# A two-block graph-attention kernel: another order for the first loads, splits and matmul passes, and twelve one-hots in two wide operations

## Chip, cores and metric

One Trainium2 chip, one core. The metric is the device time of one execution in microseconds (us). Before the change the median of 3 runs is 358.46 us (358.44 to 358.57).

## What is computed

The input is `x` (256 nodes x 768 features, float32) and 4096 edges as `src` and `dst`, sorted by `dst`. Two residual blocks follow one another, each `x = layernorm(x + block(x))`. Block 0 is a graph attention with 8 heads of 768 features and an elu behind it, then a second attention with one head. Block 1 is a 4-head attention, a layer norm, relu and residual product, then a one-head attention with the same.

```
def gat_conv(x, src, dst, W, a_src, a_dst, b, heads, out_ch):
    h = (x @ W).reshape(n, heads, out_ch)
    alpha_src = jnp.einsum('nhc,hc->nh', h, a_src)
    alpha_dst = jnp.einsum('nhc,hc->nh', h, a_dst)
    e = jax.nn.leaky_relu(alpha_src[src] + alpha_dst[dst], NEG_SLOPE)
    ...
    out = jax.ops.segment_sum(msg, dst, num_segments=n)
```

In block 0 the node itself is added as one more edge, in block 1 too. The kernel never gathers by edge. It counts once how many edges lead from node s to node d (a 256 x 256 matrix of counts), and does every attention as a dense softmax weighted with these counts.

## The kernel before

**Products in three passes.** Every float32 matrix product is made of three fp32r products: high part by high part (pass 0), high by low (pass 1) and low by high (pass 2). `product` (line 999) writes the matmuls of the passes that it is given; the tuples `ALL`, `FIRST_TWO` and `LAST_ONE` (line 526) name them. A weight chunk is 128 rows x 768 columns (384 KB). It is loaded into `raw`, a ring of three groups of two chunks. ACT copies its high part into `ring_hi` (`split_hi`, line 349), and DVE or POOL subtracts that from the raw chunk into `ring_lo` (`split_lo`, line 367). In the first phase DVE does this for chunks 0 to 3 and POOL for chunks 4 and 5; in all later phases POOL does all six. `x` is transposed on PE (`transpose_x`, line 1152), each third of its columns by itself; its high part is copied from PSUM by ACT (`input_hi`, line 700) and its low part is subtracted by DVE (`input_lo`, line 1449).

**Phases.** A phase is six chunks. Phase 0 projects `x` with head 0's weights, phase 1 with head 1's; then phases of the second attention's weights and of the next head's alternate in a loop. All order is written out by hand: each engine has one program and waits on semaphores. The engines run their programs strictly in this order.

**The start, engine by engine.**

- SP (line 560 on) issues the loads: chunk 0 of phase 0, the first third of `x`, `src`, `dst`, chunk 1, the second third, chunk 2, the last third, chunk 3, then chunks 4 and 5 as one load of 768 KB. The three loads of phase 1 follow (`load_phase`, line 540), each 768 KB: the first waits until DVE has subtracted chunk 1 (the group of `raw` is then free), the second for chunk 3, the third for POOL's chunk 5.
- PE (line 1148 on): 8 matmuls on zeros (`keep_warm`), the transposes of the first third of `x`, 2 more on zeros, then the six chunks of phase 0, with the other transposes ahead of chunks 1 and 2. Chunks 0 and 2 wait for their low part at once (`chunk`, line 1013) and do passes 0 and 1, then pass 2. Then come chunks 0 and 1 of phase 1, the counting of edges (`count_edges`, line 1184), the scores of head 0 and chunks 2 to 5 of phase 1. Ahead of the second half of the last of them stand the transposes of head 0's weights.
- ACT (line 705 on): high parts of the chunks as they land, the three `input_hi`, and twenty of the 32 step rows for the counting (`steps`, line 696), in pieces. Between them it issues two loads of the attention vectors (`load_att`, line 680) and one of a bias (line 720). Behind that come the high parts of phase 1's chunks 0 and 1 (line 839), four steps, the high part of head 0's features, chunks 2 and 3, six steps and chunks 4 and 5.
- DVE (line 1456 on): low parts of chunks 0 to 3 and of `x`, edge arithmetic, twelve steps (`late_steps`, line 1478), the 32 one-hots (`hots`, line 1460), then the dot products for head 0 (line 1504) and the unpacking of the counts (line 1677).
- POOL: constants, then the low parts of chunks 4 and 5 and of phase 1.

**Counting.** Edge tile t has 128 edges, one on each partition. Its one-hot row has, at the edge's `dst` modulo 128, a weight that says in which half of the nodes `dst` is; its step row says for each node whether it lies at or above `src`. The product of both over all 32 tiles, 257 columns wide, gives running sums whose differences are the packed counts. Before, the weight is in the one-hot, and the steps are +0.5 or -0.5 for t from 20 on:

```
dve.tensor_scalar(hot(t), iota_ps[:, 1:1 + P], row_of[:, t:t + 1], weight_of[:, t:t + 1], ALU.is_equal, ALU.mult)
dve.tensor_scalar(step(t), iota[:, :], edges_f[:, 0, t:t + 1], -0.5, ALU.is_ge, ALU.add)
```

Of the kernel before, what the change touches and what calls it, by code (L numbers as in the profile page):

```python
# [22 lines left out]
ALU = mybir.AluOpType  # L23
# [94 lines left out]
def build_gnn(nc, x, src, dst, b0_W1, b0_as1, b0_ad1, b0_b1, b0_W2, b0_as2, b0_ad2, b0_b2,  # L118
# [5 lines left out]
    with ctx:  # L124
# [96 lines left out]
        STEPS_EARLY = 5  # L221
# [8 lines left out]
        single_loaded = [sem(f"single_loaded{c}") for c in range(2)]  # L230
# [118 lines left out]
        def split_hi(eng, p, c, reused=True):  # L349

            if p is FIRST_PHASE and c in (0, 2):
                eng.wait_ge(single_loaded[c // 2], 16)
            elif c % 2 == 0 or p is FIRST_PHASE and c in (1, 3):
                eng.wait_ge(raw_full[c // 2], 16 * p + 16)
# [177 lines left out]
        def _(sp):  # L532
# [26 lines left out]

            sp.dma_start(raw[:, 0, 0:D], w1[:, 0, 0, :]).then_inc(single_loaded[0], 16)  # L560
            load_x(0)
            sp.dma_start(edges[:, 0, :], src.rearrange("(p t) -> p t", p=P)).then_inc(edges_loaded, 16)
            sp.dma_start(edges[:, 1, :], dst.rearrange("(p t) -> p t", p=P)).then_inc(edges_loaded, 16)
            sp.dma_start(raw[:, 0, D:2 * D], w1[:, 1, 0, :]).then_inc(raw_full[0], 16)
# [4 lines left out]
            load(0, 2, w1_of(0)(2))  # L569
# [109 lines left out]
        def _(act):  # L679
            def load_att(n, a_src, a_dst, width, reused=True):  # L680

                if reused:
                    act.wait_ge(a_dst_done, 2 * n)
# [23 lines left out]
            input_hi(0)  # L707
            split_hi(act, FIRST_PHASE, 1, reused=False)
            act.wait_ge(iota_cast, 1)
            act.wait_ge(src_biased, 1)  # L710
            steps(0, 3)
            split_hi(act, FIRST_PHASE, 2, reused=False)
            input_hi(1)
            steps(3, 5)
            split_hi(act, FIRST_PHASE, 3, reused=False)
            input_hi(2)
            load_att(0, b0_as1[0:1, :], b0_ad1[0:1, :], D, reused=False)
            split_hi(act, FIRST_PHASE, 4, reused=False)
# [274 lines left out]
        def _(pe):  # L993
# [26 lines left out]
            def keep_warm(times, at):  # L1020


                for _ in range(times):
                    pe.matmul(ps[:, at:at + BANK], zeros[:, 0:P], zeros[:, :], start=True, stop=True)
# [124 lines left out]
            keep_warm(8, PROJ)  # L1149
# [11 lines left out]
            keep_warm(2, PROJ + 2 * BANK)  # L1161
            for c in range(CH):
                if c == 2:
# [864 lines left out]
```

## Time and profile before

| what | value |
|---|---|
| median of 3 runs | 358.46 us |
| the profiled execution's own time | 358.43 us |
| its span in the profile | 356.6 us |
| PE busy | 347.9 us, 98% of the span |
| DVE, ACT, POOL busy | 213.4, 218.5 and 242.4 us |
| DMA | 65.15 MB, 183 GB/s over the span |

The profile is of one execution. The span goes from its first to its last instruction; 1.8 us of the execution's own time lie around it. Starts below are counted from the start of the span. "Idle" in a row is the time that the engine stood still just ahead of it, with the instruction or load that ended it.

### The profile page before, as it was taken

What the parts mean: (1) busy time and instruction counts of PE and PEld (TensorE: products, weight loads), DVE (VectorE), ACT (ScalarE), POOL (GpSimd) and SP (SyncE); (2) the same over time, 40 slices, a digit from 0 to 9 for tenths busy, and PEclk for the clock granted to TensorE, in tenths of its full rate; (3) what the DMA queues carried; (4) which work ended last, traced back from release to release, by engine and by line L of the source; (5) the groups of instructions that cost most, each with busy time, mean ns of one, the idle gap of its engine ahead of it and who ended that gap; (6) DMA issues with size and microseconds to landing.
All of it is one profiled execution on the core that took longest, in us unless ns stands there. A gap on an engine that the chain in (4) does not pass through costs nothing.

```text
span 356.6 us, 6079 instructions
## 1 busy us (share of the span) xinstructions
PE 347.9 (98%) x2058; PEld 298.9 (84%) x2060; DVE 213.4 (60%) x545; ACT 218.5 (61%) x376; POOL 242.4 (68%) x163
## 2 busy tenths in 40 slices
PE   7999999999999999999999999999999999999994
PEld 4888889889888988988898898898667888788883
DVE  4999883263546418244552732636687897944776
ACT  5987697547737754864674575476376866255601
POOL 2379769657693884968569396674257898687911
PEclk9999999999999999999999999999999999999999
DMA  7987969576656556656574754757072656246002
GB/s 235 312 299 225 391 214 257 179 240 144 227 150 203 176 155 205 170 176 183 170 217 143 224 170 141 246 159 237 11 218 94 217 179 198 99 135 221 0 2 88
DMA packets 24544, 65.15 MB, mean 183 GB/s; under 512 B 1952, under 2 KB 3024, under 8 KB 24528
## 3 DMA queue, kind: packets, MB, share of 16 engines
q1 hardware_dynamic: 20864, 55.02, 47.0%
q10 hardware_dynamic: 3664, 9.92, 10.8%
q8 instruction: 9, 0.15, 0.2%
q14 instruction: 7, 0.06, 0.0%
HBM read 64.15 MB, written 0.79 MB: 182 GB/s over the span
## 4 chain that ended last, share of the span: by engine, by line
PE 92%; DVE 4%; ACT 1%; DMA 1%; issue 1%; DVEq 0%; SPq 0%
PE ps L1008 64%; PE ps L1298 10%; PE ps L1096 9%; PE ps L1130 2%; PE ps L1362 2%; PE ps L1075 1%; DMA x_sb<-in_x 1%; PE ps L1060 1%; PE ps L1192 1%; DVE stats L1744 1%; DVE ps L1964 1%; DVE z L1971 1%; PE ps L1157 0%; PE ps L1383 0%; PE ps L1310 0%
## 5 line engine op out<-in xcount | busy, mean ns | idle before, releaser
L370 POOL TENSOR_TENSOR ring_lo<-raw,ring_hi 128x768 fp32r<-128x768 f32 x92 | 167.0, 1849 | 70.9 <-ACT ring_hi L357 70.8
L357 ACT ACTIVATE ring_hi<-raw 128x768 fp32r<-128x768 f32 x96 | 77.3, 839 | 35.7 <-PE ps L1008 28.8
L386 POOL TENSOR_TENSOR ring_lo<-raw,ring_hi 128x512 fp32r<-128x512 f32 (+1 forms) x40 | 59.5, 1517 | 20.3 <-ACT ring_hi L379 20.2
L1008 PE MATMUL ps<-ring_hi,zT_hi 128*128 128x256 f32 (+1 forms) x256 | 69.3, 345 | 0.4 <-ACT zT_hi L808 0.4
L1008 PE MATMUL ps<-ring_lo,zT_hi 128*128 128x256 f32 (+1 forms) x256 | 67.1, 337 | 0.0
L1008 PE MATMUL ps<-ring_hi,zT_lo 128*128 128x256 f32 (+1 forms) x256 | 66.8, 338 | 0.0
L1515 DVE CUSTOM_DVE_ANT_0 e<-ps,att 128x768 f32<-128x768 f32 x38 | 34.3, 953 | 47.6 <-PE ps L1008 47.6
L1008 PE MATMUL ps<-ring_hi,xT_hi 128*128 128x512 f32 x192 | 51.2, 343 | 0.3 <-ACT xT_hi L702 0.3
L1008 PE MATMUL ps<-ring_lo,xT_hi 128*128 128x512 f32 x192 | 50.0, 336 | 0.0
L1008 PE MATMUL ps<-ring_hi,xT_lo 128*128 128x512 f32 x192 | 49.8, 337 | 0.0
L1008 PEld LDWEIGHTS ps<-ring_lo,zT_hi 128*128 128x128 f32 x256 | 43.0, 188 | 5.6
L1008 PEld LDWEIGHTS ps<-ring_hi,zT_lo 128*128 128x128 f32 x256 | 43.0, 188 | 5.5
L1008 PEld LDWEIGHTS ps<-ring_hi,zT_hi 128*128 128x128 f32 x256 | 42.0, 189 | 6.4 <-ACT zT_hi L808 1.0
L379 ACT ACTIVATE ring_hi<-raw 128x512 fp32r<-128x512 f32 (+1 forms) x40 | 26.5, 712 | 17.0 <-PE ps L1008 10.0
L1657 DVE SCALAR_TENSOR_TENSOR ps<-ps,b_plus,z 128x256 f32<-128x256 f32 x48 | 21.2, 487 | 25.9 <-ACT z L800 25.8
L1008 PEld LDWEIGHTS ps<-ring_hi,xT_hi 128*128 128x128 f32 x192 | 32.3, 188 | 5.0 <-ACT xT_hi L702 0.7
L1008 PEld LDWEIGHTS ps<-ring_lo,xT_hi 128*128 128x128 f32 x192 | 32.7, 188 | 4.2
L1008 PEld LDWEIGHTS ps<-ring_hi,xT_lo 128*128 128x128 f32 x192 | 32.6, 188 | 4.1
L1096 PE MATMUL ps<-pT_hi,h_hi 128*128 128x256 f32 x96 | 26.0, 282 | 0.0
L1096 PE MATMUL ps<-pT_hi,h_lo 128*128 128x256 f32 x96 | 26.0, 282 | 0.0
L1666 DVE SCALAR_TENSOR_TENSOR zT_lo<-ps,zT_hi 128x512 fp32r<-128x512 f32 x24 | 16.6, 691 | 15.3 <-ACT zT_hi L808 15.3
L794 ACT ACTIVATE z<-ps,b_minus 128x256 f32<-128x256 f32 x48 | 20.1, 471 | 6.2 <-PE ps L1096 6.2
(172 smaller groups left out, 545.4 us busy)
## 6 DMA issues: line engine op xcount, KB each, us to landing
raw<-in_L_gnn_W SPq DMA_DIRECT2D x54, 768.0 KB, 4.5
raw<-in_L_gnn_Wr SPq DMA_DIRECT2D x8, 768.0 KB, 4.3
att<-in_L_gnn_a_src ACTq DMA_DIRECT2D x10, 384.0 KB, 4.0
att<-in_L_gnn_a_dst ACTq DMA_DIRECT2D x10, 384.0 KB, 5.2
raw<-in_L_gnn_W SPq DMA_DIRECT2D x4, 384.0 KB, 5.0
x_sb<-in_x SPq DMA_DIRECT2D x3, 256.0 KB, 4.8
rows_hc<-in_L_gnn_b SPq DMA_DIRECT2D x1, 512.0 KB, 7.6
rows_hc<-in_L_gnn_g SPq DMA_DIRECT2D x1, 512.0 KB, 8.4
```

The costliest lines, as they stand in the source:

```text
L357: eng.activation(slot_hi(c), raw_chunk(c), ACT.Copy).then_inc(hi_done, 1)
L370: eng.tensor_tensor(slot_lo(c), raw_chunk(c), slot_hi(c).bitcast(F32), ALU.subtract)\
L379: eng.activation(ring_hi[:, q["ring_at"]:q["ring_at"] + w], raw[:, q["raw_group"], q["raw_at"]:q["raw_at"] + w], ACT.Copy)\
L386: eng.tensor_tensor(ring_lo[:, q["ring_at"]:q["ring_at"] + w], raw[:, q["raw_group"], q["raw_at"]:q["raw_at"] + w], ring_hi[:, q["ring_at" ...
L794: act.activation(z[:, t * N:(t + 1) * N], ps[:, at:at + N], ACT.Relu, bias=b1_minus[:, bass.ds(KD * h + t, 1)], scale=-1.0).then_inc(elu_r ...
L1008: last = pe.matmul(ps[:, at + to:at + to + hi - lo], a, b[:, lo:hi], start=start and n == 0 and to != D, stop=stop and n == PASSES - 1, sk ...
L1096: return pe.matmul(ps[:, at:at + N], feat(features, 0, j)[:, ch:ch + P], weights_part[:, 0, j, :], start=first, stop=final, skip_group_che ...
L1130: return pe.matmul(ps[:, nat_at[i] + lo:nat_at[i] + hi], weights_part[:, 0, j, i * P:(i + 1) * P], feat(features, a, j)[:, lo:hi], start=f ...
L1298: last = pe.matmul(ps[:, to:to + HW], a, b, start=k == 0 and n == 0, stop=k == KD - 1 and n == PASSES - 1, skip_group_check=True)
L1515: dve.tensor_tensor_reduce(junk[:, at:at + w], of[:, (k - first_head(a)) * w:(k - first_head(a) + 1) * w], att[:, half_at * row + k * w:ha ...
L1657: dve.scalar_tensor_tensor(ps[:, at:at + N], ps[:, at:at + N], b1_plus[:, bass.ds(KD * h + t, 1)], z[:, t * N:(t + 1) * N], ALU.add, ALU.m ...
L1666: dve.scalar_tensor_tensor(zT_lo[:, 2 * q:2 * q + 2, :].rearrange("p k n -> p (k n)"), ps[:, at:at + 2 * N], -1.0, hi.bitcast(F32), ALU.ad ...
```

## The change

It touches the first 25 us or so of every engine but POOL. SP loads the first third of `x` ahead of chunk 0, chunk 1 ahead of the edges, chunks 4 and 5 singly, and then the attention vectors, which ACT issued before. PE issues 5 wide matmuls on zeros ahead of the transposes and 2 wide ones and one of 256 columns behind them. Chunks 0, 1 and 2 do pass 0, then pass 2, then pass 1; for chunks 1 and 2 the next transposes stand behind pass 0, and the low part of the chunk is waited for only ahead of pass 1. The high part of `x`'s first third is copied by DVE. ACT does 2 steps ahead of chunk 4 and 8 behind chunk 5 (before: 3, 2 and 5). For t from 20 on the weight is in the step, a second operand read for each partition, and the one-hots of tiles 20 to 23 and 24 to 31 are one comparison each, a `tensor_tensor` over 4 x 128 and 8 x 128 elements. The late steps are 1, 2, 3 and 6 in place of 5 and 7. One more small operation prepares the weights.

```
-        STEPS_EARLY = 5
+        STEPS_EARLY = 3
+        BELOW_FROM = (ACT_STEPS + ET) // 2
+        PLAIN = ((ACT_STEPS, 24), (24, ET))
...
-            if p is FIRST_PHASE and c in (0, 2):
+            if p is FIRST_PHASE and c % 2 == 0:
                 eng.wait_ge(single_loaded[c // 2], 16)
-            elif c % 2 == 0 or p is FIRST_PHASE and c in (1, 3):
+            elif c % 2 == 0 or p is FIRST_PHASE:
                 eng.wait_ge(raw_full[c // 2], 16 * p + 16)
...
+            load_x(0)
             sp.dma_start(raw[:, 0, 0:D], w1[:, 0, 0, :]).then_inc(single_loaded[0], 16)
-            load_x(0)
+            sp.dma_start(raw[:, 0, D:2 * D], w1[:, 1, 0, :]).then_inc(raw_full[0], 16)
             sp.dma_start(edges[:, 0, :], src.rearrange("(p t) -> p t", p=P)).then_inc(edges_loaded, 16)
             sp.dma_start(edges[:, 1, :], dst.rearrange("(p t) -> p t", p=P)).then_inc(edges_loaded, 16)
-            sp.dma_start(raw[:, 0, D:2 * D], w1[:, 1, 0, :]).then_inc(raw_full[0], 16)
             load_x(1)
...
-            load(0, 2, w1_of(0)(2))
+            sp.dma_start(raw[:, 2, 0:D], w1[:, 4, 0, :]).then_inc(single_loaded[2], 16)
+            sp.dma_start(raw[:, 2, D:2 * D], w1[:, 5, 0, :]).then_inc(raw_full[2], 16)
+            for half_at, v in ((0, b0_as1), (1, b0_ad1)):
+                sp.dma_start(att[:, half_at * D:(half_at + 1) * D], v[0:1, :].partition_broadcast(P))\
+                  .then_inc(att_loaded, 16)
             load_phase(1, w1_of(1))
...
-            input_hi(0)
             split_hi(act, FIRST_PHASE, 1, reused=False)
+            split_hi(act, FIRST_PHASE, 2, reused=False)
+            input_hi(1)
+            split_hi(act, FIRST_PHASE, 3, reused=False)
             act.wait_ge(iota_cast, 1)
             act.wait_ge(src_biased, 1)
-            steps(0, 3)
-            split_hi(act, FIRST_PHASE, 2, reused=False)
-            input_hi(1)
-            steps(3, 5)
-            split_hi(act, FIRST_PHASE, 3, reused=False)
+            steps(0, 2)
+            split_hi(act, FIRST_PHASE, 4, reused=False)
             input_hi(2)
-            load_att(0, b0_as1[0:1, :], b0_ad1[0:1, :], D, reused=False)
-            split_hi(act, FIRST_PHASE, 4, reused=False)
             split_hi(act, FIRST_PHASE, 5, reused=False)
             act.dma_start(rows_d[:, 3, :], b0_b2.partition_broadcast(P)).then_inc(b2_loaded, 16)
-            steps(5, 10)
+            steps(2, 10)
...
-            keep_warm(8, PROJ)
+            keep_warm(5, PROJ)
...
             transpose_x(0)
             keep_warm(2, PROJ + 2 * BANK)
+            keep_warm(1, PROJ + 2 * BANK, N)
             for c in range(CH):
-                if c == 2:
+                if c == 3:
                     pe.wait_ge(b1_loaded, 16)
...
-                if c in (1, 2):
-                    transpose_x(c)
-                if c in (0, 2):
+                if c in (0, 1, 2):
                     pe.wait_ge(xT_hi_done, c // 2 + 1)
-                    chunk(FIRST_PHASE, c)
-                    for passes in (FIRST_TWO, LAST_ONE):
+                    pe.wait_ge(hi_done, c + 1)
+                    for passes in ((0,), LAST_ONE, (1,)):
                         if passes is LAST_ONE:
+                            if c > 0:
+                                transpose_x(c)
                             pe.wait_ge(xT_lo_done, c // 2 + 1)
+                        if passes == (1,):
+                            chunk(FIRST_PHASE, c)
...
+            def plain_hots(first, end):
+                at = (first % per_home) * 2 * N
+                home = hot_homes[first // per_home][:, at:at + (end - first) * 2 * N]
+                shape = [P, end - first, P]
+                dve.tensor_tensor(home.rearrange("p (t n) -> p t n", n=2 * N)[:, :, 0:P],
+                                  iota_ps[:, 1:1 + P].rearrange("p (t n) -> p t n", t=1).to_broadcast(shape),
+                                  row_of[:, first:end].rearrange("p (t n) -> p t n", n=1).to_broadcast(shape),
+                                  ALU.is_equal).then_inc(hot_done, 1)
...
+            dve.wait_ge(xT_ps, 1)
+            dve.tensor_copy(xT_hi[:, 0:2, :].rearrange("p k n -> p (k n)"), ps[:, XT_AT:XT_AT + BANK])\
+               .then_inc(xT_hi_done, 1)
+            input_lo(0)
             split_lo(dve, FIRST_PHASE, 0)
-            input_lo(0)
...
-            for at, end, scale in ((0, ACT_STEPS, 1.0), (ACT_STEPS, ET, 2.0)):
+            for at, end, scale in ((0, ACT_STEPS, 1.0), (ACT_STEPS, BELOW_FROM, 2.0), (BELOW_FROM, ET, -2.0)):
...
-                    dve.tensor_scalar(step(t), iota[:, :], edges_f[:, 0, t:t + 1], -0.5, ALU.is_ge, ALU.add)\
-                       .then_inc(step_dve_done, 1)
+                    dve.tensor_scalar(step(t), iota[:, :], edges_f[:, 0, t:t + 1], weight_of[:, t:t + 1],
+                                      ALU.is_lt if t >= BELOW_FROM else ALU.is_ge, ALU.mult).then_inc(step_dve_done, 1)
...
-            hots(0, ET)
+            hots(0, ACT_STEPS)
+            for first, end in PLAIN:
+                plain_hots(first, end)
```

## Rows read from the trace of the kernel before

**Rows 1.** The page: busy time, share of the span and instructions by engine.

```profile
PE 347.9 (98%) x2058; PEld 298.9 (84%) x2060; DVE 213.4 (60%) x545; ACT 218.5 (61%) x376; POOL 242.4 (68%) x163
```

**Rows 2.** Chain that ended last, in order of time: start us, us, what.

```profile
1.19 3.88 DMA x_sb<-in_x
...
12.34 12.58 PE ps L1008 x72
```

**Rows 3.** Timeline, head: start us, us, engine, line, operation, tiles, count, idle.

```profile
1.31 3.59 PE L1024 MATMUL ps<-zeros 128*128 128x512 bf16 x8 [1.31 <-POOL zeros L601]
...
4.37 0.84 ACT L357 ACTIVATE ring_hi<-raw 128x768 fp32r<-128x768 f32 x1 [2.13 <-DMA raw<-in_L_gnn_W]
...
5.20 0.72 PE L1157 MATMUL ps<-ident,x_sb 128*128 128x128 f32 x4 [0.30 <-DMA x_sb<-in_x]
...
5.76 0.59 PE L1024 MATMUL ps<-zeros 128*128 128x512 bf16 x2
5.96 0.60 ACT L702 ACTIVATE xT_hi<-ps 128x512 fp32r<-128x512 f32 x1 [0.76 <-PE ps L1157]
...
6.62 0.62 PE L1008 MATMUL ps<-ring_hi,xT_hi 128*128 128x512 f32 x2 [0.26 <-ACT xT_hi L702]
...
7.07 0.51 PE L1008 MATMUL ps<-ring_lo,xT_hi 128*128 128x512 f32 x2
```

**Rows 4.** Timeline, PE: first matmuls of phase 1 and of the counting.

```profile
20.55 0.51 PE L1008 MATMUL ps<-ring_hi,xT_hi 128*128 128x512 f32 x2
...
24.76 1.05 PE L1192 MATMUL ps<-am 128*128 128x257 bf16 x8
```

**Rows 5.** Timeline, ACT and POOL: last splits of phase 0, steps, first of phase 1.

```profile
14.03 0.83 ACT L357 ACTIVATE ring_hi<-raw 128x768 fp32r<-128x768 f32 x1
...
14.28 7.26 POOL L370 TENSOR_TENSOR ring_lo<-raw,ring_hi 128x768 fp32r<-128x768 f32 x4 [11.00 <-ACT ring_hi L357]
...
14.77 1.30 ACT L698 ACTIVATE am<-iota,src_bias 128x257 bf16<-128x257 bf16 x3
...
16.77 1.56 ACT L357 ACTIVATE ring_hi<-raw 128x768 fp32r<-128x768 f32 x2
```

**Rows 6.** DMA issues: chunk 3 (at 4.57), phase 1's first (at 9.17): us to landing.

```profile
raw<-in_L_gnn_W SPq DMA_DIRECT2D x1, 384.0 KB, 6.3
...
raw<-in_L_gnn_W SPq DMA_DIRECT2D x1, 768.0 KB, 5.6
```

**Rows 7.** Windows: us, busy time by engine, PEclk, DMA share, GB/s.

```profile
4.50:5.00 0.50, 0.41 (x1) 0.00 (x0) 0.00 (x0) 0.50 (x1) 0.00 (x0) 1.00 0.90 156
...
12.00:13.00 1.00, 1.00 (x10) 0.91 (x8) 1.00 (x7) 0.70 (x2) 0.00 (x0) 1.00 1.03 409
...
15.00:16.00 1.00, 1.00 (x8) 0.89 (x7) 1.00 (x5) 1.00 (x4) 1.00 (x1) 1.00 0.89 135
16.00:17.00 1.00, 1.00 (x7) 0.85 (x6) 1.00 (x5) 1.00 (x4) 1.00 (x2) 1.00 1.02 187
...
39.00:40.00 1.00, 1.00 (x10) 1.00 (x10) 1.00 (x3) 0.78 (x2) 1.00 (x1) 1.00 1.03 422
```

**Rows 8.** DMA issues: second attention vector (at 12.77): us to landing.

```profile
att<-in_L_gnn_a_dst ACTq DMA_DIRECT2D x1, 384.0 KB, 7.0
```

**Rows 9.** Groups by line and shape, DVE: busy us, mean ns.

```profile
L1693 DVE TENSOR_SCALAR far<-ps 128x256 f32<-128x256 f32 x2 | 0.8, 418 | 0.0
...
L1622 DVE TENSOR_SCALAR am<-ps,rz 128x256 f32<-128x256 f32 x16 | 7.0, 479 | 0.3
...
L1451 DVE TENSOR_TENSOR xT_lo<-ps,xT_hi 128x512 fp32r<-128x512 f32 x3 | 2.1, 685 | 0.4 <-ACT xT_hi L702 0.4
```

**Rows 10.** Timeline, DVE: last one-hots, first dot product, first unpacking step.

```profile
19.77 5.19 DVE L1462 TENSOR_SCALAR rows_hc<-ps,row_of,weight_of 128x128 bf16<-128x128 f32 x16
...
24.88 0.95 DVE L1515 CUSTOM_DVE_ANT_0 e<-ps,att 128x768 f32<-128x768 f32 x1
...
29.25 0.41 DVE L1677 SCALAR_TENSOR_TENSOR hs<-hs,ps 128x256 f32<-128x256 f32 x1
```

More of the change, by code:

```diff
@@ L229, in build_gnn @@
         chunk_used = sem("chunk_used")
-        single_loaded = [sem(f"single_loaded{c}") for c in range(2)]
+        single_loaded = [sem(f"single_loaded{c}") for c in range(RG)]
         x_loaded = [sem(f"x_loaded{b}") for b in range(3)]
@@ L679, in _, with load_att @@
         def _(act):
-            def load_att(n, a_src, a_dst, width, reused=True):
-                if reused:
-                    act.wait_ge(a_dst_done, 2 * n)
+            def load_att(n, a_src, a_dst, width):
+                act.wait_ge(a_dst_done, 2 * n)
                 for half_at, v in ((0, a_src), (1, a_dst)):
@@ L1018, in node_tile, with keep_warm @@
                 return t[:, k, i * P:(i + 1) * P]
-            def keep_warm(times, at):
+            def keep_warm(times, at, width=BANK):
                 for _ in range(times):
-                    pe.matmul(ps[:, at:at + BANK], zeros[:, 0:P], zeros[:, :], start=True, stop=True)
+                    pe.matmul(ps[:, at:at + width], zeros[:, 0:P], zeros[:, 0:width], start=True, stop=True)
             def project_chunk(p, h, c, loop=False, at=PROJ, between=None):
@@ L1186, in count_edges @@
                 for t in range(ET):
-                    pe.wait_ge(hot_done, t + 1)
+                    pe.wait_ge(hot_done, t + 1 if t < ACT_STEPS else ACT_STEPS + sum(first <= t for first, _ in PLAIN))
                     if t < ACT_STEPS:
@@ L1479, in late_steps @@
                 for t in range(first, end):
-                    dve.tensor_scalar(step(t), iota[:, :], edges_f[:, 0, t:t + 1], -0.5, ALU.is_ge, ALU.add)\
-                       .then_inc(step_dve_done, 1)
+                    dve.tensor_scalar(step(t), iota[:, :], edges_f[:, 0, t:t + 1], weight_of[:, t:t + 1],
+                                      ALU.is_lt if t >= BELOW_FROM else ALU.is_ge, ALU.mult).then_inc(step_dve_done, 1)
             split_lo(dve, FIRST_PHASE, 1)
             dve.wait_ge(iota_cast, 2)
-            late_steps(ACT_STEPS, ACT_STEPS + STEPS_EARLY)
+            dve.wait_ge(edges_split, 5)
+            late_steps(ACT_STEPS, ACT_STEPS + 1)
             split_lo(dve, FIRST_PHASE, 2)
             input_lo(1)
-            late_steps(ACT_STEPS + STEPS_EARLY, ET)
+            late_steps(ACT_STEPS + 1, ACT_STEPS + STEPS_EARLY)
             split_lo(dve, FIRST_PHASE, 3)
+            late_steps(ACT_STEPS + STEPS_EARLY, ACT_STEPS + 2 * STEPS_EARLY)
             input_lo(2)
+            late_steps(ACT_STEPS + 2 * STEPS_EARLY, ET)
             dve.wait_ge(b1_ps, 1)
@@ L1494, in _ @@
                .then_inc(b1_ready, 1)
-            dve.wait_ge(edges_split, 4)
-            hots(0, ET)
+            hots(0, ACT_STEPS)
+            for first, end in PLAIN:
+                plain_hots(first, end)
             def dots_scale(a, half_at, i):
```

## Prediction

> **What bounds the kernel now.** Read first the page's busy times: PE is busy for 98% of the span [rows 1], so nothing but less work or less standing on PE can shorten it. PE's work stays the same but for 2.5 matmuls on zeros, which stand ahead of the first product. So the question is how much earlier PE gets through the head, and whether it keeps that. The chain that ended last starts with the load of `x`'s first third, issued at 1.19 us and landed 3.88 us later, at 5.07, and from 12.34 on it is PE without a gap [rows 2]. The timeline of the head shows what lies between: transposes at 5.20, the copy of their high part on ACT at 5.96 for 0.60 us, the first product at 6.62 [rows 3]. Chunk 0 itself had landed at 4.37, when ACT started its split. So the first product waits for `x`, not for the weights. Further marks are PE's start of phase 1 at 20.55 and of the counting at 24.76 [rows 4]. For what PE would meet if it came earlier I read ACT and POOL [rows 5] and the DMA issues and windows [rows 6 to 8].
>
> **Step 1, the first product: 0.65 us earlier.** `x`'s first third and chunk 0 change places. Together they have landed at 5.07 now, so chunk 0 as the second should land at about 5.07. Its split takes 0.84 us, to 5.91, and PE follows its releaser by 0.06 (5.96 + 0.60 = 6.56, against 6.62) [rows 3]: 5.97. The other leg must be no later. 256 KB cannot land later than 384 KB in the same place do, at 4.37. Plus 0.13 to the transposes (5.07 to 5.20), 0.76 to the copy (5.20 to 5.96), and the copy on DVE. No row has this copy; DVE's subtraction of the same 512 columns takes 685 ns [rows 9] and reads one tensor more, so I take 0.69, with ACT's 0.60 as the near bound. That is 5.95 at the latest, so the leg is covered. The low parts come in the order `x` (to about 6.6), then chunk 0 (to about 7.5); PE wants them one and two passes in, at 6.8 and 7.5. That is even, because the pass that needs the later one comes last. Three matmuls fewer on zeros cost nothing in themselves; see the clock below.
>
> **Step 2, PE from there to phase 1: 0.10 us longer.** Now 13.93 us lie between the first product and phase 1 (6.62 to 20.55). A pair of matmuls that starts after something else takes 0.45 us (6.62 to 7.07) in place of 0.35 [rows 3]. The transposes inside chunks 1 and 2 make such a restart each, as the ones ahead of them do now; the bias transpose, now next to the last ones, gets a restart of its own. So 14.03, and PE is at phase 1 at 20.00 instead of 20.55: 0.55 earlier. Chunks 3 to 5 are covered by what step 3 works out for ACT: chunk 3 is split from 10.5 on, so its low part is ready near 12.7 and wanted near 13.7; POOL's two are ready near 14.7 and 16.5 and wanted near 15.8 and 17.9.
>
> **Step 3, ACT and POOL up to phase 1: just in time.** PE needs the low part of phase 1's chunk 0. ACT starts its high part at 16.77 [rows 5], and POOL does its four low parts in 7.26 us, so in 1.82 each, the third ready at 19.75. After the change ACT has eight steps behind chunk 5 in place of five. Its work from chunk 3 on: split 0.74 (14.03 to 14.77), two steps at 0.40 (five take 14.77 to 16.77), split 0.74, copy 0.60, split 0.74, eight steps 3.20: 6.82 in all. Chunk 3 now lands at 4.57 + 6.3 = 10.87 [rows 6]. The same bytes stand ahead of it afterwards, but the DMA engines have a dip to 156 GB/s at 4.5 to 5.0 us [rows 7], while the two small edge loads pass, and large loads stood behind these. With chunk 1 ahead of them part of the dip is filled. Bounds: nothing gained, 10.87, or the dip's whole 0.7 us, 10.2; I take the middle, 10.5. Then phase 1's first split starts at 17.3, POOL can begin at 18.15 and has done at 20.0. PE arrives at 20.0, so I charge 0.08. With the bounds it is nothing to 0.45.
>
> **Step 4, the load of phase 1.** It is issued at 9.17 and lands 5.6 us later, at 14.77 [rows 6], two microseconds ahead of its use. Now 768 KB of attention vectors go ahead of it in SP's own queue. At 409 GB/s (12 to 13 us) that is 1.9 us; at the 135 and 187 GB/s of 15 to 17 us, when those vectors move now [rows 7], it is 4.9. So it lands between 14.77 + 1.9 - 0.3 (half the dip) = 16.4 and 19.4. SP's own broadcasts of the later bias rows run at 422 GB/s at 39 to 40 us [rows 7], so I take the near end plus 0.6, a part of the 0.9 us that a third 384 KB takes, for the bias load from ACT beside it, 17.0: ahead of ACT's 17.3, free. The attention vectors themselves, landed at 12.77 + 7.0 = 19.8 now [rows 8], are wanted at about 23.6, and ACT saves two issues in its program.
>
> **Step 5, the counting.** DVE has run without idling from 7.2 us to the first unpacking step at 29.25 and stands in the way of the head's softmax, which PE reaches just in time. It loses twelve one-hots at 5.19/16 = 0.32 us [rows 10], 3.89 us, and gains two wide comparisons. The nearest row is the subtraction of 512 elements, 0.69 [rows 9]; two to three times that for 512 and 1024 elements together is 1.4 to 2.1, and I take 1.8. The second operand per partition makes each late step longer: 479 ns with one against 418 with none on the same shape [rows 9], 0.06, or 0.7 us for twelve (bounds: 0 and 0.1 each). The third weight operation adds 0.1. Net 3.9 - 1.8 - 0.7 - 0.1 = 1.3 us earlier: one-hots end at 23.6 instead of 24.9, and all DVE does behind them can follow. That covers PE's gain; without the wide ones DVE would now be 0.8 late and PE would wait for it. ACT's last steps need 17.3 + two splits 1.5 + four steps 1.6, then the features behind chunk 5, 1.5, two splits, 1.5, six steps, 2.4: 25.8. PE wants the last at about 26.4. Covered.
>
> **Sum.** 0.65 - 0.10 - 0.08 = 0.47 us at phase 1. I take off 0.1 for small new waits behind it, and all that comes later is a chain on PE which shifts as a whole. Against the profiled execution's 358.43 that gives 358.06; the median stands 0.03 above it. Forecast: **358.1 us**. A measurement of this kernel tells about 0.2%, 0.72 us, from no change, so this is within it.
>
> **Rival 1, slower: the load of phase 1 lands late.** If the vectors move at the slow rate of 15 to 17 us, the load lands at 18.8 or later instead of 17.0. From 17.3 on each 0.1 us of it is 0.1 on ACT, POOL and PE. At 17.8 the gain is gone; at 18.8 PE starts phase 1 at 18.8 + 0.84 + 1.84 + 0.06 = 21.5, 1.0 later than now: 359.4 us. For it: 135 GB/s at a DMA share of 0.89 [rows 7]. Against it: in those windows they go through the other queue. The Trainium skill (DMA: Bandwidth & Descriptors, Queues, rings and completion order) says that each engine takes its queues in turn and drains one queue in order; by that rule the vectors, until now beside SP's loads, are ahead of them, and the trace agrees so far, since phase 1's first load lands ahead of both vectors now.
>
> **Rival 2, slower: the clock comes later.** The eight matmuls of 512 columns on zeros start 0.43 us apart, 512 at 1.2 GHz; the two at 5.76 are at 0.21, so at 2.4 GHz [rows 3]. PE had then worked from 1.31 to 4.90 and again from 5.20. Afterwards the zeros end at about 3.6, PE stands until about 4.2, and works again. If the clock is still at 1.2 GHz at the first product, a pass costs 1.28 us (two node tiles of 768 columns) instead of 0.70: for chunk 0's three passes 1.7 us, so 359.8; with two passes it is already 0.2% slower than now. The Trainium skill (TensorE: Matmul & The Clock Gate, Part 1) says the array is throttled by default, that sustained activity releases it, and that the moment varies from run to run, which speaks against cutting the work on zeros. The four times before lie within 0.14 us, which does not show such a variation.
>
> **Rival 3, nothing moves.** The gain of the head is swallowed by chunk 3 landing at 10.87 and by POOL: PE waits 0.45 at phase 1, 358.3 to 358.5. **Rival 4, more:** the second landing is earlier, the dip is filled, and PE's small stutters go as well: 0.8 to 1.0, 357.5.
>
> **Chances.** Forecast 0.50, of which 0.08 may lie beyond 0.72 us; rival 1 0.18 (half of it over 0.2% slower), rival 2 0.13 (0.10 over it), rival 3 0.11, rival 4 0.08 (all faster). Faster 0.16, slower 0.19 and 0.02 for mishaps, 0.21; within 0.2% 0.63. The range leaves out the far ends of rivals 1 and 2 and of 4: 357.5 to 359.2.
>
> **What would show it.** Right: first product at about 5.95, phase 1 on PE near 20.1, counting near 24.3, dot products on DVE near 23.6, no PE wait over 0.2 us, everything behind shifted by 0.4. Wrong: matmuls 0.43 us apart beyond 6 us (rival 2); ACT idle for the weights near 17 us and PE idle at phase 1 (rival 1); late steps well over 0.34 us or the wide comparisons over 2.1 us together, with PE waiting in the counting; or a PE gap behind 30 us.

## The result, and the profile after

The changed kernel takes 360.26 us (median of 6 runs, 359.97 to 361.14), the kernel before 358.61 beside it (6 runs, 358.44 to 358.74). The ratio is 1.0048, 95% interval 1.0036 to 1.0061: slower by 1.7 us. The forecast was 358.1, in a range of 357.5 to 359.2. The profiled execution took 360.47 us.

The page of the changed kernel, busy times and the chain that ended last:

```profile
span 358.7 us, 6069 instructions
...
PE 347.9 (97%) x2056; PEld 299.0 (83%) x2058; DVE 215.4 (60%) x537; ACT 218.2 (61%) x375; POOL 242.6 (68%) x163
...
PE 84%; DVE 11%; ACT 2%; DMA 1%; issue 1%; DVEq 0%; SPq 0%
```

PE's work is what it was, 347.9 us [rows 1]. But DVE has 2.0 us more work. It should have had 0.6 less: the forecast's 1.3 us, less the 0.7 of the copy of `x`'s first third, which it takes over from ACT. Its share of the last chain is 11%. In the kernel before it was 4%, and PE had the chain without a gap from 12.34 to 24.92 [rows 2] and on to the transposes of head 0's weights. A line of its page, and one of its timeline:

```profile
PE 92%; DVE 4%; ACT 1%; DMA 1%; issue 1%; DVEq 0%; SPq 0%
...
36.04 0.60 PE L1075 MATMUL ps<-ident,am 128*128 128x128 f32 x4
```

Which of PE's waits is new? The waits of the changed kernel, costliest first:

```profile
PE ps L1078 <- DVE am L1645: 1.4, 1, 1.4
PE ps L1027 <- POOL zeros L609: 1.3, 1, 1.3
PE ps L1012 <- ACT ring_hi L361: 0.8, 1, 0.8
```

The first is new and carries the loss: PE stands 1.4 us ahead of the transposes of head 0's weights, which DVE's softmax delivers. The chain from there back, in order of time (start, us, what):

```profile
11.88 0.86 DVE ring_lo L374
12.74 2.31 DVE rows_hc L1499 x3
15.05 0.59 DVE xT_lo L1457
15.65 2.51 DVE rows_hc L1499 x6
...
18.38 2.55 DVE am L1478 x8
```

Line 1499 is a late step of the counting. Three take 2.31 us and six take 2.51; before, five took 1.07 and seven 1.47. The timeline of the head, DVE, POOL and PE:

```profile
12.66 2.40 DVE L1499 TENSOR_SCALAR rows_hc<-iota,edges_f,weight_of 128x257 bf16<-128x257 bf16 x3
14.97 0.68 DVE L1457 TENSOR_TENSOR xT_lo<-ps,xT_hi 128x512 fp32r<-128x512 f32 x1
15.57 2.59 DVE L1499 TENSOR_SCALAR rows_hc<-iota,edges_f,weight_of 128x257 bf16<-128x257 bf16 x6
...
24.66 1.84 DVE L1471 TENSOR_TENSOR rows_hc<-ps,row_of 128x512 bf16<-128x512 f32 x2
26.38 0.97 DVE L1538 CUSTOM_DVE_ANT_0 e<-ps,att 128x768 f32<-128x768 f32 x1
...
13.06 3.72 POOL L374 TENSOR_TENSOR ring_lo<-raw,ring_hi 128x768 fp32r<-128x768 f32 x2 [9.76 <-ACT ring_hi L361]
18.14 3.65 POOL L374 TENSOR_TENSOR ring_lo<-raw,ring_hi 128x768 fp32r<-128x768 f32 x2 [1.36 <-ACT ring_hi L361]
...
6.53 0.94 PE L1012 MATMUL ps<-ring_hi,xT_hi 128*128 128x512 f32 x4 [0.80 <-ACT ring_hi L361]
...
24.66 1.05 PE L1198 MATMUL ps<-am 128*128 128x257 bf16 x8
...
37.52 0.66 PE L1078 MATMUL ps<-ident,am 128*128 128x128 f32 x4 [1.43 <-DVE am L1645]
```

Both slow groups lie beside POOL's pair of subtractions, 13.06 to 16.78. In the kernel before the late steps stood here:

```profile
9.06 1.07 DVE L1480 TENSOR_SCALAR rows_hc<-iota,edges_f 128x257 bf16<-128x257 bf16 x5
...
11.60 1.47 DVE L1480 TENSOR_SCALAR rows_hc<-iota,edges_f 128x257 bf16<-128x257 bf16 x7
```

The last of them ended at 13.07 (11.60 + 1.47), and POOL's first subtraction started at 14.28 [rows 5]: they never met. In single instructions (min/median/max) the twelve are

```profile
L1499 DVE TENSOR_SCALAR rows_hc<-iota,edges_f,weight_of x12: 342/347/1883, 9.0 to 17.8; 128x257 bf16<-128x257 bf16 x12
```

Ten take 0.35 us, one takes 1.88 (issued at 13.17, 0.1 us after POOL began) and one 1.30 (issued at 15.57, ending at 16.87, 0.1 us behind POOL's second subtraction). That is 1.53 + 0.95 = 2.5 us too much. DVE reaches its first dot product at 26.38 instead of 24.88 [rows 10], 1.50 later, the weights' transposes start at 37.52 instead of 36.04, 1.48 later, and PE does not make it up. Theory A: **a late step that meets a subtraction of POOL stands until that ends, inside its own recorded duration**, and DVE's lateness becomes PE's.

### The profile page after: what moved, and what is told of

It is laid out like the page before. It is cut to its first block, busy times and chain, and to the rows that moved or that the text cites. A ratio compares the mean times of both kernels' runs of the same rounds, so it can differ in the third digit from the quotient of the medians.

```text
span 358.7 us, 6069 instructions
## 1 busy us (share of the span) xinstructions
PE 347.9 (97%) x2056; PEld 299.0 (83%) x2058; DVE 215.4 (60%) x537; ACT 218.2 (61%) x375; POOL 242.6 (68%) x163
## 4 chain that ended last, share of the span: by engine, by line
PE 84%; DVE 11%; ACT 2%; DMA 1%; issue 1%; DVEq 0%; SPq 0%
PE ps L1012 58%; PE ps L1304 10%; PE ps L1099 9%; PE ps L1133 2%; PE ps L1368 2%; PE ps L1078 2%; DVE rows_hc L1499 1%; DMA raw<-in_L_gnn_W 1%; PE ps L1063 1%; DVE e L1538 1%; DVE stats L1767 1%; DVE am L1478 1%; DVE z L1478 1%; DVE ps L1987 1%; DVE z L1994 1%
## 5 line engine op out<-in xcount | busy, mean ns | idle before, releaser
L383 ACT ACTIVATE ring_hi<-raw 128x512 fp32r<-128x512 f32 (+1 forms) x40 | 26.5, 713 | 17.1 <-PE ps L1012 10.3
```

The costliest lines, as they stand in the source:

```text
L383: eng.activation(ring_hi[:, q["ring_at"]:q["ring_at"] + w], raw[:, q["raw_group"], q["raw_at"]:q["raw_at"] + w], ACT.Copy)\
```

## The experiments

Each ran beside the kernel before on its chip. "Dots" is the start of DVE's first dot product; "1.0028 [1.0018, 1.0038]" is a ratio to the kernel before, with its 95% interval.

**e1: the late steps read the copy of the node numbers in PSUM.** All else is the changed kernel.

```
-                    dve.tensor_scalar(step(t), iota[:, :], edges_f[:, 0, t:t + 1], weight_of[:, t:t + 1],
+                    dve.tensor_scalar(step(t), iota_ps, edges_f[:, 0, t:t + 1], weight_of[:, t:t + 1],
```

> The changed kernel, with the twelve late steps reading the row of node numbers from its PSUM copy instead of SBUF. Theory A (a late step reads and writes SBUF in a fast form that cannot run beside POOL's SBUF subtraction, and waits until that one ends): read from PSUM no late step is longer than 0.6 us, the 1.88 and 1.30 us ones are gone; each costs some 0.20 us more by itself (a 257-column PSUM operation took 0.42, plus two operands of 0.06), so 2.4 us are added where 2.5 go, the dot products start near 26.3 us as now, and the time stays at 360.0 to 360.5. Theory B (the long steps come from something else: the second operand, or the DMA writes into SBUF): the two long ones stay at 1.9 and 1.3, 2.4 us come on top, 362 to 363.

360.0 us, 1.0028 [1.0018, 1.0038]. The line of the late steps (instructions: min/median/max ns, first and last start), and two rows of the timeline:

```profile
L1499 DVE TENSOR_SCALAR rows_hc<-ps,edges_f,weight_of x12: 540/544/549, 8.9 to 17.0; 128x257 bf16<-128x257 f32 x12
```

```profile
12.96 3.65 POOL L374 TENSOR_TENSOR ring_lo<-raw,ring_hi 128x768 fp32r<-128x768 f32 x2 [9.68 <-ACT ring_hi L361]
14.71 2.81 DVE L1499 TENSOR_SCALAR rows_hc<-ps,edges_f,weight_of 128x257 bf16<-128x257 f32 x6
```

Beside the same pair of subtractions no step is long. All cost 0.54 instead of 0.35 for the other source, so more than half of the loss stays: dots at 25.76. The copy in PSUM is float32 and the one in SBUF bfloat16, so this edit changes place and type at once; which of the two frees the step is not shown.

**e2: the old one-hots and the old late steps, in the new places.** The hunks of the diff on `plain_hots`, `weight_of` and `late_steps` are undone; the order stays.

> The changed kernel with the old one-hots (32 narrow, weighted) and the old steps (one operand per partition and -0.5), in the new places. Theory A (waiting for POOL): two of the late steps still take 1.9 and about 1.3 us, the others 0.28; DVE loses the 1.3 us that the wide ones save, the dot products start near 27.7 and the time is 361.2 to 361.9. Theory B (the second operand is what makes late steps long): all late steps take 0.28, the dot products start near 25.2, 358.6 to 359.2.

363.8 us, 1.0151 [1.0125, 1.0177]. The steps have a minimum of 0.28, a median of 0.29 and a maximum of 1.89 us; the long ones start at 14.34 (0.98) and 15.23 (1.89), beside POOL's pair at 13.37. So the long steps come from the place, not from the second operand. Dots are at 28.27. The time is above what was expected, since DVE is now so late that PE waits in three more places: 1.5 us for the scores, 1.3 for the next phase's input, 0.5 for POOL.

**e3: the late steps kept clear of POOL.** Two, one and three ahead of the low part of chunk 3, six behind the seventh one-hot, between POOL's two pairs.

```
-            late_steps(ACT_STEPS, ACT_STEPS + 1)
+            late_steps(ACT_STEPS, ACT_STEPS + 2)
             split_lo(dve, FIRST_PHASE, 2)
+            late_steps(ACT_STEPS + 2, ACT_STEPS + 3)
             input_lo(1)
-            late_steps(ACT_STEPS + 1, ACT_STEPS + STEPS_EARLY)
+            late_steps(ACT_STEPS + 3, ACT_STEPS + 6)
             split_lo(dve, FIRST_PHASE, 3)
-            late_steps(ACT_STEPS + STEPS_EARLY, ACT_STEPS + 2 * STEPS_EARLY)
             input_lo(2)
-            late_steps(ACT_STEPS + 2 * STEPS_EARLY, ET)
...
-            hots(0, ACT_STEPS)
+            hots(0, 7)
+            late_steps(ACT_STEPS + 6, ET)
+            hots(7, ACT_STEPS)
```

> The changed kernel with its late steps where POOL stands: 2, 1 and 3 of them ahead of chunk 3's low part, which ends as POOL starts, and 6 behind the seventh one-hot, in POOL's pause from 16.8 to 18.1 us. Theory A: at most one step over 0.5 us, dot products start near 24.0 us instead of 26.4, PE no longer waits 1.4 us at the transposes of head 0's weights, the time is 358.3 to 358.7, so that of the kernel before. Theory B (the late steps or the wide comparisons cost too much in themselves, wherever they stand): 360 or more. If the order of loads and passes at the head was a gain in itself, it shows here as less than 358.4.

358.48 us, 0.9985 [0.9976, 0.9994]. Repeated as e14 below: 0.9986. Its late steps by line, and its timeline:

```profile
L1499 DVE TENSOR_SCALAR rows_hc<-iota,edges_f,weight_of x12: 341/346/349, 8.8 to 17.7; 128x257 bf16<-128x257 bf16 x12
```

```profile
16.44 1.64 DVE L1499 TENSOR_SCALAR rows_hc<-iota,edges_f,weight_of 128x257 bf16<-128x257 bf16 x6
...
18.08 3.64 POOL L374 TENSOR_TENSOR ring_lo<-raw,ring_hi 128x768 fp32r<-128x768 f32 x2 [1.42 <-ACT ring_hi L361]
...
23.86 0.95 DVE L1539 CUSTOM_DVE_ANT_0 e<-ps,att 128x768 f32<-128x768 f32 x1
24.29 1.05 PE L1198 MATMUL ps<-am 128*128 128x257 bf16 x8
```

The same twelve instructions take 3.5 us in all in place of 5.9, dots start 2.5 earlier than in the changed kernel, the new wait of PE is gone, and the time falls by 2.2 us, to below the kernel before. The place of the late steps alone makes the difference between a loss and a gain. The first of the six still starts 0.22 us ahead of the end of POOL's first pair (14.82 + 1.84), but it is no longer than the others: it ends at 16.78, 0.1 behind POOL.

**e4: the kernel before with the wide comparisons and the weighted steps, all else in its old place.**

```
-            hots(0, ET)
+            hots(0, ACT_STEPS)
+            for first, end in PLAIN:
+                plain_hots(first, end)
```

(The hunks on `plain_hots`, `weight_of` and the steps themselves, as in the change, are left out here.)

> The kernel before with only the DVE part of the change: weight in the late steps, twelve one-hots in two comparisons, the late steps in their old places (5 and 7), all of them ahead of POOL's first subtraction at 14.3 us. Theory A: no long step, the dot products start near 23.6 instead of 24.9, PE does not need them earlier, time unchanged within 0.2 us of 358.6. If instead DVE was what PE waited for in the head: up to 1 us faster.

359.02 us, 1.0003 [0.9994, 1.0012]. Steps 346 to 354 ns, dots at 23.57, 1.3 us earlier than in the kernel before; DVE then stands 1.49 us ahead of its first unpacking step. PE does not gain, as it was bound by its own work.

**e5: the kernel before with seven of its late steps moved behind the low part of `x`'s last third.** Nothing of the change is in it.

```
-            late_steps(ACT_STEPS + STEPS_EARLY, ET)
             split_lo(dve, FIRST_PHASE, 3)
             input_lo(2)
+            late_steps(ACT_STEPS + STEPS_EARLY, ET)
```

> The kernel before, with one thing moved: its seven late steps stand behind the low part of x's last third, so from about 13.1 us on, and run into POOL's run of four subtractions from 14.3 to 21.5 us; nothing else is changed and the work is the same. Theory A (a late step that meets a running POOL subtraction waits for its end): three or four steps fit ahead of 14.3, each later one is let in at one of POOL's boundaries (16.1, 17.9, 19.8, 21.5), so three or four steps of 1.0 to 1.9 us, DVE 5 to 6 us late at its dot products (near 30 us), PE waits for the one-hots, the scores and the weights, 363 to 365 us. Theory B (the order of DVE's work does not matter, or the long steps need the changed kernel's second operand or its DMA traffic): all steps 0.28 us, 358.9 to 359.3, as the kernel before.

364.54 us, 1.0154 [1.0137, 1.0171]. Its line of the late steps and the timeline, with the single ones cut out of their group:

```profile
L1480 DVE TENSOR_SCALAR rows_hc<-iota,edges_f x12: 283/291/1898, 9.2 to 18.2; 128x257 bf16<-128x257 bf16 x12
```

```profile
16.38 1.90 DVE L1480 TENSOR_SCALAR rows_hc<-iota,edges_f 128x257 bf16<-128x257 bf16 x1
18.20 1.88 DVE L1480 TENSOR_SCALAR rows_hc<-iota,edges_f 128x257 bf16<-128x257 bf16 x1
...
16.34 1.84 POOL L370 TENSOR_TENSOR ring_lo<-raw,ring_hi 128x768 fp32r<-128x768 f32 x1
18.15 1.83 POOL L370 TENSOR_TENSOR ring_lo<-raw,ring_hi 128x768 fp32r<-128x768 f32 x1
```

The two long steps shown start 0.04 to 0.05 us behind a subtraction and end 0.1 behind its end. Back to back, POOL lets one step in for each of its own. Three such steps (14.57, 16.38, 18.20) put dots at 30.38, 5.5 us late, and the time is 5.55 above the kernel before: one for one. The two subtractions shown are 1.83 and 1.84 us, no longer than elsewhere (mean 1.85). As the loads are those of the kernel before, the changed order of the DMAs is no cause of the long steps either.

**e6, e7, e8: the other parts of the change, one undone at a time, on top of e3.** e6 loads the edges ahead of chunk 1 again, e7 has eight wide matmuls on zeros in front again, e8 lets ACT issue the attention vectors again, behind the high part of `x`'s last third.

```
-            sp.dma_start(raw[:, 0, D:2 * D], w1[:, 1, 0, :]).then_inc(raw_full[0], 16)
             sp.dma_start(edges[:, 0, :], src.rearrange("(p t) -> p t", p=P)).then_inc(edges_loaded, 16)
             sp.dma_start(edges[:, 1, :], dst.rearrange("(p t) -> p t", p=P)).then_inc(edges_loaded, 16)
+            sp.dma_start(raw[:, 0, D:2 * D], w1[:, 1, 0, :]).then_inc(raw_full[0], 16)
```

> The kernel with late steps clear of POOL, and the two edge loads issued ahead of chunk 1, as in the kernel before. If chunk 0 lands late because chunk 1 follows it directly and shares the DMA engines: chunk 0 lands 0.3 to 0.5 us earlier (3.6 us after issue or less), chunk 1 about 0.5 later, first product near 5.7; chunk 1's high part is then wanted at 7.9 and ready at 8.1, so the time is within 0.3 us of the kernel without this edit. If its landing only varies from run to run: no difference in its landing and 0 to 0.5 us slower through chunk 1.

358.97 us, 0.9997 [0.9988, 1.0007], so 0.5 slower than e3 against its own chip's kernel before. ACT starts chunk 1 at 7.42 instead of 6.60 and phase 1 at 18.20 instead of 17.17, and PE waits 0.5 for POOL: chunk 1 ahead of the edges is worth about that by the medians, though the two intervals overlap.

```
-            keep_warm(5, PROJ)
+            keep_warm(8, PROJ)
```

> The kernel with late steps clear of POOL and 8 instead of 5 wide matmuls on zeros at the start. They end at 4.9 instead of 3.6 us, the transposes of x's first third come 1.2 us later, the copy and its low part too. If the first product runs at the lower clock because PE did less before (rival 2 of the prediction): the first four product matmuls are 0.35 us a pair here against up to 0.46, and the time is 0.1 to 0.3 us lower. If not: x's copy ends at 6.6 instead of 5.6 and PE starts its product at 6.6 instead of 5.9, 0.3 to 0.7 us slower.

358.79 us, 0.9997 [0.9988, 1.0006]. The transposes start at 4.70 in place of 3.76, behind the zeros, and the first product at 6.42 in place of 5.84. Fewer zeros are no loss; by the medians they give 0.4 us, though the two intervals overlap.

```
-            for half_at, v in ((0, b0_as1), (1, b0_ad1)):
-                sp.dma_start(att[:, half_at * D:(half_at + 1) * D], v[0:1, :].partition_broadcast(P))\
-                  .then_inc(att_loaded, 16)
...
             split_hi(act, FIRST_PHASE, 4, reused=False)
             input_hi(2)
+            for half_at, v in ((0, b0_as1), (1, b0_ad1)):
+                act.dma_start(att[:, half_at * D:(half_at + 1) * D], v[0:1, :].partition_broadcast(P))\
+                   .then_inc(att_loaded, 16)
```

> The kernel with late steps clear of POOL, and the two attention vectors issued by ACT behind the last third of x again, not by SP ahead of phase 1. Rival 1 of the prediction (they hold up phase 1's first load): that load lands near 14.8 instead of 17.0 us, but ACT is not ready for it before 17.1, and two issues cost ACT 0.3 us: phase 1's first split at 17.4 instead of 17.1, its low part on POOL at 20.2 where PE wants it at 20.0, so 0.1 to 0.4 us slower. If the load was what ACT waited for at 17.1: 0.3 us faster or more.

358.30 us, 0.9984 [0.9971, 0.9998], not to be told from e3. Phase 1's first load lands 5.9 us after its issue instead of 8.2, but ACT comes to it no earlier (17.71 in place of 17.17, and PE waits 0.5 us for POOL in the profile). Rival 1's late load costs nothing.

**e9 to e11: the changed kernel again, and the dose.** e9 is the changed kernel as it is. e10 and e11 are e3 with one and two of its last six steps put back behind the low part of `x`'s last third.

> The changed kernel as it is, beside the two variants below and the kernel before. Nothing is edited; it asks whether the lateness of chunk 0 in the first profile (landed at 5.54 us) belongs to the change or to that execution. Theory A (the end is set by DVE, which waits for POOL's subtractions): the time is again 1.0045 to 1.006 of the kernel before, even where chunk 0 lands at 4.7 to 4.9 and the first product starts at 5.7 to 5.9, since DVE's late steps are again the long ones (one of about 1.9 us, one of 1.2 to 1.8), the dot products start at 25.9 to 26.5 and PE stands 1.2 to 1.5 us for the weights' transposes. Rival B (the late landing of chunk 0 made a good part of the loss): with an early landing the ratio falls to 1.003 or less.

360.08 us, 1.0039 [1.0025, 1.0053], below the expected 1.0045 though its interval reaches it. Chunk 0 lands at 4.99 instead of 5.54, the first product starts at 5.98, dots at 26.16, and PE waits 1.4 us for the weights' transposes again. The six steps behind `x`'s last third take

```profile
14.10 3.81 DVE L1499 TENSOR_SCALAR rows_hc<-iota,edges_f,weight_of 128x257 bf16<-128x257 bf16 x6
```

where in e3 six take 1.64. This time the three ahead got through before POOL's first; the six pay for both. So the loss does not need the late landing of the first profile. There the last chain does start with that landing, but its dots came only 0.22 us later than here, and the two ratios, 1.0048 and 1.0039, are not apart.

```
             input_lo(2)
+            late_steps(ACT_STEPS + 6, ACT_STEPS + 7)
...
-            late_steps(ACT_STEPS + 6, ET)
+            late_steps(ACT_STEPS + 7, ET)
```

(e10; in e11 the bound is `ACT_STEPS + 8`.)

> The order that keeps the late steps clear of POOL, with one single step moved back behind the low part of x's last third, so that it is issued at about 14.0 us, in the middle of POOL's first subtraction (13.0 to 14.9). Theory A1 (a step that meets a subtraction of POOL stands until that subtraction ends, and costs what is left of it): this step takes about 0.95 us (14.0 to 14.9 and a bit), not 1.9, all others 0.35; the dot products start at 24.4 to 24.6 in place of 23.86, PE waits at most 0.2 to 0.3 us for the weights' transposes, and the time is 358.5 to 358.9 (ratio 0.9985 to 0.9995). Rival A2 (two engines share a port and each goes slower in proportion): the step takes 0.5 to 0.7 and POOL's subtraction grows by some 0.2. Rival A3 (a step beside POOL costs a fixed 1.9): it takes 1.9, dots at 25.4, 359.6.

> The same with two steps moved back. Theory A1: the first takes about 0.95 us, the second is issued as POOL's second subtraction starts and takes 1.8 to 1.9, until that ends at about 16.7; the dot products start at 25.9 to 26.2, 2.1 to 2.3 later than with none, PE waits 1.3 to 1.8 us for the weights' transposes, and the time is 359.9 to 360.4 (ratio 1.0025 to 1.0045): two misplaced steps of 0.35 us make nearly all of the loss of the changed kernel. Rival A2: 0.6 us each, dots at 24.4, 358.6.

362.96 us (360.14 to 364.77), 1.0102 [1.0064, 1.0140], and 363.22 us, 1.0123 [1.0106, 1.0140]. Both times were far above what was expected, though the size of the single wait was right. The timeline of e10:

```profile
13.90 0.97 DVE L1499 TENSOR_SCALAR rows_hc<-iota,edges_f,weight_of 128x257 bf16<-128x257 bf16 x1
...
15.02 2.32 DVE L1478 TENSOR_SCALAR am<-ps,row_of,weight_of 128x128 bf16<-128x128 f32 x7
17.25 4.59 DVE L1499 TENSOR_SCALAR rows_hc<-iota,edges_f,weight_of 128x257 bf16<-128x257 bf16 x5
18.01 3.73 POOL L374 TENSOR_TENSOR ring_lo<-raw,ring_hi 128x768 fp32r<-128x768 f32 x2 [1.43 <-ACT ring_hi L361]
...
27.63 0.95 DVE L1540 CUSTOM_DVE_ANT_0 e<-ps,att 128x768 f32<-128x768 f32 x1
```

The step that meets POOL in the middle takes 0.97 us, as theory A1 had it (0.95), not 1.9 and not 0.6. In e11 two take 2.77 (0.95 + 1.85 = 2.8 expected). What the expectation missed is what comes behind: 0.6 us of lateness pushes the last two of the other five past 18.0, where POOL's second pair starts. These two take 1.96 and 1.94 us, and the five 4.59 instead of 1.38. It is the forecast's own fault in small: I priced the step that I moved, and not what the ones behind it would meet. In e3 the last step starts at 17.73 and POOL's second pair at 18.08: 0.35 us to spare, less than the 0.6.

**e12, e13: more room.** e12 is e3 with one of the six behind the low part of chunk 3, where DVE stands idle for 0.58 us in e3. In e13 that one step reads PSUM.

```
             split_lo(dve, FIRST_PHASE, 3)
+            late_steps(ACT_STEPS + 6, ACT_STEPS + 7)
             input_lo(2)
...
-            late_steps(ACT_STEPS + 6, ET)
+            late_steps(ACT_STEPS + 7, ET)
```

> The order that keeps the late steps clear of POOL, with one of its last six steps put behind the low part of chunk 3, where DVE stands 0.58 us until ACT has copied x's last third; five stay behind the seventh one-hot. In the order with six, the last of them was issued at 17.7 us and POOL's next two subtractions started at 18.08: the gap between POOL's two pairs is hit with some 0.1 us to spare. Theory A (a step that is issued before POOL's subtraction starts goes ahead at its own 0.35; one issued later stands until the subtraction ends): the single step starts at about 12.7, 0.3 ahead of POOL, and takes 0.35; the five end at 17.7, the margin becomes about 0.35, the dot products start at 23.6, PE waits for none of them, since it is then bound by its own work, and the time stays 358.3 to 358.6 (ratio 0.9978 to 0.9992) with no run above 359.1. Rival (12.7 is already too near to POOL's start at 12.9 to 13.1): the single step takes 1.9 to 2.2, everything behind slips by 1.6, the five then meet the second pair, and the time is 361 to 363.

The median is 358.69 us; the ratio, which also counts the one outlier, is 1.0009 [0.9986, 1.0033]: unclear. Ten executions lie at 357.86 to 358.98, one at 363.20. In the profiled one (357.86) the single step starts at 12.60 and POOL at 12.74: 0.14 to spare, not the expected 0.3, and dots are at 23.37.

> The order with one step behind the low part of chunk 3 and five behind the seventh one-hot, with that one step alone reading the copy of the node numbers that lies in PSUM. It takes 0.54 in place of 0.35 us, in a place where DVE would stand anyhow. Theory A (the one execution at 363.2 came from this step meeting POOL's first subtraction, which pushes the five under the second pair): no execution above 359.2, the median 358.2 to 358.6, ratio 0.998 to 0.9995; the dot products start at 23.4 to 23.7, and PE waits for none of them. Rival (the five meet the second pair by themselves, or something else makes such an execution): one execution in ten or so is again at 361 or above.

358.47 us (358.20 to 359.23, 12 runs), 0.9991 [0.9982, 0.9999]. No execution is above 359.3. The step takes 0.54 in the idle time and dots start at 23.53. That fits the reading that e12's outlier was the single step meeting POOL and pushing the rest under the second pair, but it was one execution and not a profiled one: with one in eleven, twelve without prove little. It stays likely, not shown.

> The order with six steps behind the seventh one-hot, repeated. In the first profile of it the last of the six had been issued at 17.7 us, POOL's second pair started at 18.08. Theory A: the margin holds in most executions, the median is again 358.3 to 358.7 (ratio 0.998 to 0.9995); where POOL's pair comes earlier or the steps later by over 0.3 us, the last step stands 1.5 us longer, which PE feels by about 1.2: then 359.5 to 360, in at most one or two of ten. Rival (the order is no real gain): ratio 1.000 or more.

358.24 us (357.98 to 359.10, 12 runs), 0.9986 [0.9977, 0.9996]: e3's result again. No other variant is faster beyond the noise (e8, with the same late steps, has 0.9984). This order is 0.6 us under the kernel before and about 2 under the changed one.

## Why the forecast was wrong

**Step 5 is the step that failed.** It took the late steps as longer by 0.06 us each, and concluded "1.3 us earlier: one-hots end at 23.6 instead of 24.9, and all DVE does behind them can follow". It priced them by duration alone, as if a place in DVE's program were as good as any other. Step 3 of the same forecast had ACT split chunks 4 and 5 earlier, and so POOL subtract them earlier; step 2 took from it that POOL's first low part would be ready near 14.7, hence started near 12.9 (it was 13.06), and never laid the moved steps beside it. The start of POOL at 14.28 and the end of the late steps at 13.07 both stood in the profile of the kernel before. What the runs showed instead is 2.5 us of waits in the steps (5.9 us against 3.5 in e3), dots at 26.38 and 26.16, not 23.6, and a PE wait of 1.4.

**How DVE's lateness reaches PE** can be read off the profiles. The weights' transposes start 11.1 us after dots wherever PE waits for them: 26.38 to 37.52, 25.76 to 36.87 (e1), 28.27 to 39.36 (e2), 26.16 to 37.28 (e9), 27.63 to 38.74 (e10), 28.01 to 39.12 (e11). In the kernel before it is 24.88 + 11.1 = 36.0 against PE's 36.04: no slack at all. In e3 PE is there at 35.38, so dots may start until 24.3, and started at 23.86: 0.4 to spare. The forecast said "just in time" in words, and had no row for how little that was. Of the 2.5 us, 1.0 were eaten by what the new work and order had won on DVE (dots at 23.86 in e3 against 24.88) and the rest went to the end: 1.5 at 37 us, and 1.7 in the medians.

**The sizes within the step were right.** The wide comparisons take 1.84 together (forecast 1.8). The second operand costs 0.06: 346 and 349 ns in e3 and e4, against 291 in e5 with one operand.

**Steps 1 and 2** hold in the runs where they can be seen. The first product starts at 5.84 in e3 and 5.98 in e9 (forecast 5.97), and phase 1 on PE at 19.98 in e3 (20.00 before waits). In the first profile of the changed kernel chunk 0 landed at 5.54, 4.3 us after its issue, against 4.61 to 4.99 in twelve other profiles with `x`'s first third ahead; there the first product came at 6.53, so step 1 missed in that execution. By the dots of e9 that is some 0.2 us of the loss; the rest does not need it.

**Steps 3 and 4** hold too. Phase 1's first load landed at 17.1 (9.13 + 8.0; forecast 17.0), ACT started its split at 17.22 (17.3), POOL began at 18.14 (18.15), and no PE wait for POOL is in the list. Rival 1 is out by e8. Rival 2 is out as a loss by e7, though by the spacing of the matmuls the clock did come later: the zeros behind the transposes did run 0.4 us apart with five in front (three in 1.20 us, three in 0.70 with eight), but then the first four matmuls of the product took 1.08 us in e3 and 1.41 in e6, against 0.97 in e7, and with five zeros they start 0.6 earlier. Rival 3 is out too: chunk 3 was split from 10.53 on (forecast 10.5). Rival 4, 0.8 to 1.0 us faster, did not come in e3 or e14 either: without the waits the order gives 0.57 us, against 0.40 in the forecast. The sum of the forecast was right for a kernel whose late steps meet nobody, and that is e3, not this change.

**No rival had the mechanism.** "Late steps well over 0.34 us, with PE waiting in the counting" stood among the signs of being wrong, and was what came, with PE's wait 11 us further on; it had neither a price nor a chance.

## What to carry to other kernels

When an engine's operations are moved, or another engine is made to start earlier, lay the two timelines over each other in the new order, and ask for each pair of VectorE and GpSimd operations that come to overlap whether they may run together; a VectorE operation that meets a GpSimd subtraction from SBUF costs what is left of it. Then ask again for what stands behind it: the lateness can push the next ones under the next subtraction, so that 0.6 us become 3.8. Where a VectorE operation had to stand there, a float32 source in PSUM made it immune here, for 0.19 us more each.

## What the runs showed of the hardware that was not expected

**A wait that is no idle time.** A step of 0.35 us is recorded with up to 1.9 us of busy time, and neither the idle column nor the list of waits shows anything. The mean of its group does: 554 ns in place of 345, and a maximum five times the median. All sixteen profiles agree: steps with an SBUF source are long only beside POOL's subtractions (1.88 and 1.30; 1.90 and 1.88 in e5), never when they read PSUM (0.54 in e1), and DVE's subtraction `xT_lo`, whose sources are one in PSUM and one in SBUF, takes 0.68 beside POOL too. Whoever is first goes: in e12 the step at 12.60 took 0.35, 0.14 us ahead of POOL.

The Trainium skill (SBUF — State Buffer, Who interferes with whom) says that VectorE and GpSimd share one pair of SBUF ports as an exclusive lock, held for a whole instruction, that `tensor_scalar` is among the operations that can take it, that one with at most one SBUF input outside the two-port modes does not, and that the order of issue decides who waits. The traces agree that a `tensor_scalar` stands for what is left of a subtraction, and that the one issued first goes, with the numbers above; which mode a step runs in, no trace shows. By that rule the moved steps would have been a rival of their own, on the slower side. The same page allows that GpSimd is the one that waits. The traces hint at it: POOL's first subtraction takes 2.00 us in e4, where it starts 0.29 us ahead of the end of DVE's own subtraction of chunk 3, and 1.90 to 1.92 where a late step from SBUF still has 0.2 us to go (the first profile, e5, e12), against 1.85 in e13, where that step reads PSUM.

**The second source.** A late step on the same 257 columns takes 0.54 us with the numbers in PSUM as float32 and 0.35 with them in SBUF as bfloat16.

**A clock row that does not tell all.** The granted clock is shown as 1.00, the 2.4 GHz level, in every stretch from 1.5 us on, before and after, while the matmuls of 512 columns on zeros stand 0.43 us apart at first, as at 1.2 GHz, and 0.21 later [rows 3]. In the first microseconds of this kernel the clock is read from that spacing.
